# The second attention of a fused transformer kernel: softmax weights as the stationary tile, sums divided per token

## The chip, the cores and the metric

The kernel runs on one core of a Trainium2 chip. A core has a matrix engine (TensorE, PE in the profile; its weight loads are listed apart as PEld), a vector engine (VectorE, DVE), a scalar engine (ScalarE, ACT), a general engine (GpSimd, POOL) and a queue that only issues transfers (SyncE, SP). The engines run at the same time and meet at semaphores. The metric is the device time of one execution in microseconds (us); lower is better.

## The reference

Four layers are computed, each with a gated cross-attention and a gated feed-forward part. The change lies in the cross-attention of the second layer alone:

```python
# B, NQ, D = 32, 56, 128; context: 32 x 1500 x 96; 16 heads of 64
q = (x @ Wq).reshape(B, Nq, h, dh)
k = (context @ Wk).reshape(B, Nk, h, dh)
v = (context @ Wv).reshape(B, Nk, h, dh)
scores = jnp.einsum('bqhd,bkhd->bhqk', q, k) * scale
attn = jax.nn.softmax(scores, axis=-1)
out = jnp.einsum('bhqk,bkhd->bqhd', attn, v).reshape(B, Nq, h * dh)
return out @ Wo + bo
```

`Nk` is 1500 and `Nq` is 56, so each batch has 16 x 56 = 896 pairs of head and query. A pair of head and query is called a token here, as in the title of the change.

## The kernel before

`attention_wide` folds the weights so that keys and values are never projected. `Wq` and `Wk` are merged into one matrix per head, `M`, so a folded query is 96 wide and is multiplied with the raw context; `Wv` and `Wo` are merged into `N` (96 x 128 per head), so the softmax weights are applied to the raw context as well, and the 96-wide result is projected by `N` afterwards.

The 32 batches are taken in two halves of 16, each by one call of `attend_wide`; a half is eight pairs of batches (`NP` = 8), the inner batches of a pair being `s` = 0 and 1. `pairs` writes the first pair out, loops over the middle ones, and writes the last one out. Each pair has 24 steps (12 for each batch); a step is one tile of 125 keys. On PE a step `k` of `body` consists of:

- `chunks`: while `k % 12 < 11`, two (at the eleventh one) products of 128 folded queries with 500 keys of the *next* pair, in PSUM banks 6 and 7. DVE takes their maxima (`chunk_max`, line 1512); the maxima make the shift of the softmax. PE waits before each for the maximum of the one before.
- `score`: six products of 448 columns for the tile two steps ahead (lines 1333 to 1335): keys stationary, all 896 folded queries moving, split in two halves of 448, three products each for precision. ACT exponentiates them into the tile `P` (125 keys x 896 tokens, line 1494).
- `weigh`: two products (line 1347) with the context rows `CN` (125 keys x 97: 96 features and a column of ones) stationary and the 448 columns of `P` moving. The sums stay in banks 4 and 5 as 97 x 896 over twelve steps; row 97 is the softmax's denominator.
- `make_image`: in six of the 24 steps, a product of 500 columns for another layer, in bank 7.
- `project`: once per pair, at step 10, sixteen products of 112 columns (line 1318), `N[0:DC, h, :]` stationary and the normalised sums `UN` moving, into bank 6. `aside` places it. ACT's `out` copies the result into `OT`.

After a batch's twelfth step its sums are normalised: `copy_sums` (ACT, line 1428) copies 97 x 896 into `UE`; SP sends row 97 as 8 x 112 values into spare rows of `qp` (line 1211); DVE's `invert` takes reciprocals (line 1525); SP sends them to device memory (line 1213) and reads them back broadcast over 96 partitions into `RB` (line 1215); POOL's `norm` multiplies (line 1260). Because `project` comes some ten steps later, this runs beside the next batch's steps, except behind the last pair of each half, where `project(NP - 1)` stands alone at the end.

All matmul operands of `weigh` and `project` are float32; the profile shows each such instruction as two records (768 products of `weigh` are 1536 records). The order on each engine is that in which the code is written; nothing is scheduled automatically. Line numbers are those of the profile.

## Time and profile before

| | us |
|---|---|
| median of 3 runs | 4144.75 (4140.34 to 4147.81) |
| the profiled execution | 4137.59 |
| its span, first to last instruction | 4136.0 |
| PE busy in it | 3638.2 (88%) |
| DVE, ACT, POOL busy | 2430.1, 2047.4, 1527.6 |

The steps of the second attention run from about 1209 us of the span to 2529, its last projection to 2546. The busy share of a whole kernel says little, since stages differ; what matters is which engine has no gap where this attention runs, and what one instruction costs there. A matmul record is longer than the time after which the next one starts (they are pipelined): the spacing has to be read from a run of them, as (length of the run - length of one) / (count - 1).

### The profile page before, as it was taken

How to read it: one execution, taken by the hardware profiler on the slowest of the kernel's cores; microseconds unless marked ns; L12 is line 12 of the kernel's file. 1: busy time of each engine (PE TensorE's matmuls, PEld its weight loads, DVE VectorE, ACT ScalarE, POOL GpSimd, SP SyncE). 2: the span in 40 equal slices, each digit the busy share in tenths (PEclk: the TensorE clock that was granted, in tenths of full speed). 3: DMA queues.
4: the chain of work that ended last, by engine and by line, in shares of the span. 5: the costliest groups of instructions: out<-in, count | busy, mean ns of one | idle time of the engine just before them, and what ended most of it. 6: DMA issues, size and time to landing. Idle time of an engine off the chain costs nothing. (4 is left out here: it accounts for less than half of the span.)

```text
span 4136.0 us, 84598 instructions
## 1 busy us (share of the span) xinstructions
PE 3638.2 (88%) x33128; PEld 2481.3 (60%) x33128; DVE 2430.1 (59%) x3802; ACT 2047.4 (50%) x2959; POOL 1527.6 (37%) x1887
## 2 busy tenths in 40 slices
PE   8499999946489999989999997679958799999997
PEld 8367777733366666666666665257733366666664
DVE  7556666543245554515454542467644799999993
ACT  8177777711134443434443442166422377777764
POOL 5265545221423233213323220022201577666651
PEclk9699999968789999999999997889969699999998
DMA  6177777546223332213333220021000566666650
GB/s 188 49 170 178 176 167 175 145 182 235 52 71 90 84 91 81 80 51 87 81 87 87 83 78 26 10 64 46 13 19 16 123 145 144 140 140 147 145 120 15
DMA packets 202294, 421.94 MB, mean 102 GB/s; under 512 B 51993, under 2 KB 108244, under 8 KB 201844
## 3 DMA queue, kind: packets, MB, share of 16 engines
q1 hardware_dynamic: 131524, 327.92, 31.2%
q0 software_dynamic: 34944, 46.10, 5.1%
q10 hardware_dynamic: 35504, 43.39, 3.9%
q8 instruction: 231, 3.78, 0.4%
q14 instruction: 91, 0.75, 0.1%
HBM read 232.39 MB, written 32.56 MB: 64 GB/s over the span
## 5 line engine op out<-in xcount | busy, mean ns | idle before, releaser
L1512 DVE TENSOR_REDUCE L_mp<-ps 128x2 f32<-128x1000 f32 (+1 forms) x352 | 402.4, 1151 | 560.7 <-PE ps L1310 557.3
L1347 PE MATMUL ps<-L_p,L_cn 125*97 125x448 f32 x1536 | 639.2, 538 | 0.0
L1494 ACT ACTIVATE L_p<-ps 125x896 f32<-125x896 f32 x384 | 352.1, 917 | 533.8 <-PE ps L1335 462.5
L2291 DVE TENSOR_REDUCE L_mp<-ps 112x1 f32<-112x500 f32 x726 | 454.2, 667 | 64.5 <-PE ps L2040 64.4
L1333 PE MATMUL ps<-L_qh,L_ch 97*125 97x448 f32 x768 | 384.4, 501 | 0.0
L1347 PEld LDWEIGHTS ps<-L_p,L_cn 125*97 125x97 f32 x1536 | 250.4, 163 | 199.9 <-issue 165.9
L2241 ACT ACTIVATE L_p<-L_p 125x896 f32<-125x896 f32 x256 | 243.3, 950 | 178.6 <-DVE L_p L2308 178.0
L2308 DVE TENSOR_SCALAR L_p<-ps 125x896 f32<-125x896 f32 x256 | 276.5, 1080 | 24.6 <-PE ps L2061 24.5
L920 ACT ACTIVATE L_p<-ps,rk 125x896 f32<-125x896 f32 x256 | 257.7, 1007 | 50.9 <-PE ps L776 46.8
L1334 PE MATMUL ps<-L_ql,L_ch 96*125 96x448 f32 x768 | 282.3, 368 | 0.0
L1335 PE MATMUL ps<-L_qh,L_cl 96*125 96x448 f32 x768 | 280.8, 366 | 0.0
L2040 PE MATMUL ps<-L_ks,L_qs 96*128 96x500 bf16 x768 | 246.3, 396 | 28.2 <-DMA L_qs<-L_q_part 12.4
L1310 PE MATMUL ps<-L_cr,L_qb 96*128 96x500 f32 x672 | 234.7, 427 | 17.3 <-POOL L_qb L1235 17.3
L2061 PEld LDWEIGHTS ps<-L_qs,L_ks 128*128 128x128 bf16 x3072 | 191.0, 99 | 71.5 <-issue 46.4
L776 PEld LDWEIGHTS ps<-L_qs,L_ks 128*128 128x128 bf16 x3072 | 188.0, 98 | 72.9 <-issue 54.6
L2074 PE MATMUL ps<-L_p,L_vs 125*18 125x112 f32 x6144 | 224.1, 264 | 7.2 <-POOL L_p L1923 5.3
L1260 POOL TENSOR_TENSOR L_un<-L_ue,L_rb 96x896 f32<-96x896 f32 x32 | 67.2, 2099 | 424.3 <-DMA L_rb<-L_den 424.3
L692 POOL TENSOR_TENSOR L_k_part<-L_k_rest,L_k_part 128x500 bf16<-128x500 f32 x96 | 109.2, 1139 | 299.4 <-ACT L_k_part L885 299.4
L2061 PE MATMUL ps<-L_qs,L_ks 128*128 128x112 bf16 x3072 | 217.2, 214 | 2.8 <-DVE L_mp L2286 1.5
L776 PE MATMUL ps<-L_qs,L_ks 128*128 128x112 bf16 x3072 | 216.1, 213 | 3.4 <-ACT L_p L920 3.4
L702 POOL DMA_DIRECT2D L_qs<-L_q_part x384 | 214.2, 566 | 7.6 <-DVEq L1042 6.8
L945 DVE COPY L_vs<-ps 125x384 f32<-125x384 f32 x128 | 70.9, 554 | 232.4 <-PE ps L752 232.2
(538 smaller groups left out, 7632.6 us busy)
## 6 DMA issues: line engine op xcount, KB each, us to landing
L_ks<-L_k_part SPq DMA_DIRECT2D x288, 375.0 KB, 6.1
L_ks<-L_k_first SPq DMA_DIRECT2D x96, 375.0 KB, 5.2
moe_w<-in_L_w SPq DMA_DIRECT2D x64, 512.0 KB, 6.6
L_cn<-in_ctxN SPq DMA_DIRECT2D x32, 568.4 KB
cs_ct<-in_ctxT SPq DMA_DIRECT2D x32, 562.5 KB, 4.2
L_cr<-in_ctxT POOLq DMA_DIRECT2D x32, 562.5 KB
L_ch<-in_ctxT POOLq DMA_DIRECT2D x32, 562.5 KB, 4.5
L_raw<-in_ctxT SPq DMA_DIRECT2D x32, 562.5 KB, 5.1
```

Of the source, the lines that this page charges most:

```text
L776: mm = nc.tensor.matmul(SB[n % 2][:, m // 4, m % 4 * 2 * NQ:(m % 4 + 1) * 2 * NQ] .rearrange("p (j q) -> p j q", j=2), KS[b.r % 3][:, k0:k ...
L920: nc.scalar.activation(weights_at[n % 3][0:KP, :].rearrange("p (a n) -> p a n", a=2), SB[n % 2][0:KP], ACT.Exp, scale=rk[:, b.lin(KT, n):b ...
L1333: nc.tensor.matmul(SB[n % 2][:, a, :], CH[s][:, k], QH[s][:, q], start=True, stop=False)
L1334: nc.tensor.matmul(SB[n % 2][:, a, :], CH[s][0:DC, k], QL[s][:, q], start=False, stop=False)
L1335: mm = nc.tensor.matmul(SB[n % 2][:, a, :], CL[s][:, k], QH[s][0:DC, q], start=False, stop=True)
L1347: mm = nc.tensor.matmul(U[:, a, :], CN[s][:, j, :], P[:, n % 2, a * HALF:(a + 1) * HALF], start=(j == 0), stop=(j == KT - 1))
L1494: nc.scalar.activation(two(P[:, n % 2, :]), SB[n % 2], ACT.Exp).then_inc(S["exped"].sem, 1)
L1512: nc.vector.tensor_reduce(mp[:, 2 * k:2 * k + n], ps[:, bank:bank + n, 0:500], AX.X, ALU.max).then_inc(S["chunk_maxed"].sem, 1)
L2040: nc.tensor.matmul(ps[:, CB[pair].start + a, 0:500], QS[b.r % 4][0:96, m * 2 * NQ:m * 2 * NQ + 128], KS[b.r % 4][0:96, m * NK + p * 500:m ...
L2061: mm = nc.tensor.matmul(SB[n % 2][:, m // 4, m % 4 * 2 * NQ:(m % 4 + 1) * 2 * NQ] .rearrange("p (j q) -> p j q", j=2), KS[b.r % 4][:, k0:k ...
L2291: nc.vector.tensor_reduce(mp[:, 2 * c + a:2 * c + a + 1], ps[0:TT, CB[0].start + a, 0:500], AX.X, ALU.max).then_inc(S["chunk_maxed"], 1)
L2308: nc.vector.tensor_scalar(two(P[0:KP, n % 3, :]), SB[n % 2][0:KP], 0.0, -RANGE, ALU.min, ALU.max).then_inc(S["clipped"], 1)
```

## The change

What is stationary and what moves is exchanged in `weigh`. Each step now has seven products (`QT` = 7): 128 tokens of `P` are the stationary tile, and the 97 columns of `CN` move. The sums lie as 128 tokens x 97 in seven places, four in bank 4 and three in bank 5 (`weighed_sum`). So the denominator of a token is on the token's own partition, in column 97:

- `copy_sums` is split: ACT copies the four places of bank 4 (388 columns), DVE the three of bank 5 (291 columns).
- `invert` is one DVE reciprocal of 128 x 7, straight from `UE`; the three transfers of SP, `RB` and the device buffer `den` are gone.
- `norm` on POOL multiplies 128 x 672 with the reciprocals broadcast along the features, into `UT`.
- `project` needs features on partitions, so `turn` transposes the seven tiles of a batch on PE (96 x 128 each, into banks 6 and 7), and `copy_turned` copies them into `UN`, 512 columns by ACT and 384 by DVE. `turn` stands at step 10 (for the batch before) and step 22 (for the first of the pair), behind waits for banks 6 and 7; `project` moves to step 11, ACT's `out` to `n == 13`. At the end of a half `turn` and `copy_turned` stand before the last `project`.

```diff
-    UE = sb("ue", [KA, HQ])
-    UN = sb("un", [DC, H, 2, NQ])
+    UE = sb("ue", [128, QT, KA])
+    UT = sb("ut", [128, QT, DC])
+    UN = sb("un", [DC, 2, HQ])
+    rc = sb("rc", [128, QT])
...
-    U = ps[0:KA, 4:6, 0:HALF]
+    def weighed_sum(t):
+        return ps[:, 4 + t // 4, t % 4 * KA:(t % 4 + 1) * KA]
...
             def norm(i, s):
-                pool.wait_ge(*at("den_in", 32 * i + 16 * s + 16))
-                nc.gpsimd.tensor_tensor(UN[:, :, s, :], heads(UE[0:DC, :]), heads(RB[:, :]), ALU.mult
-                                        ).then_inc(S["u_normed"].sem, 1)
+                pool.wait_ge(*at("den_inverted", 2 * i + s + 1))
+                pool.wait_ge(*at("u_turned", 2 * i + s + 1))
+                nc.gpsimd.tensor_tensor(UT[:, :, :], UE[:, :, 0:DC], rc[:, :].unsqueeze(2).to_broadcast([128, QT, DC]),
+                                        ALU.mult).then_inc(S["u_normed"].sem, 1)
...
+            def turn(i, s):
+
+                pe.wait_ge(*at("u_normed", 2 * i + s + 2))
+                for t in range(QT):
+                    mm = nc.tensor.transpose(ps[0:DC, 6 + t // 4, t % 4 * 128:(t % 4 + 1) * 128], UT[:, t, :],
+                                             core.ident[:, :])
+                mm.then_inc(S["u_turned"].sem, 1)
+
             def project(i):
 
-                pe.wait_ge(*at("u_normed", 2 * i + 3))
+                pe.wait_ge(*at("un_low_copied", 2 * i + 2))
+                pe.wait_ge(*at("un_high_copied", 2 * i + 2))
...
-                for a in range(2):
-                    mm = nc.tensor.matmul(U[:, a, :], CN[s][:, j, :], P[:, n % 2, a * HALF:(a + 1) * HALF],
-                                          start=(j == 0), stop=(j == KT - 1))
+                for t in range(QT):
+                    mm = nc.tensor.matmul(weighed_sum(t), P[:, n % 2, t * 128:(t + 1) * 128], CN[s][:, j, :],
+                                          start=(j == 0 and t % 4 == 0),
+                                          stop=(j == KT - 1 and t in (3, QT - 1)))
...
             def aside(i, k, prev, nxt):
 
-                if k == 10 and prev:
+                if (k == 10 and prev) or k == 22:
+                    pe.wait_ge(*at("img_kept", 6 * i + (3 if k == 10 else 6)))
                     if nxt:
                         pe.wait_ge(*at("chunk_maxed", 2 * CG * i + 2 * CG + groups_by(k)))
+                    else:
+                        pe.wait_ge(*at("chunk_maxed", 2 * CG * i + 2 * CG))
+                if k == 10 and prev:
+                    turn(i - 1, 1)
+                if k == 11 and prev:
                     project(i - 1)
+                if k == 22:
+                    if prev:
+                        pe.wait_ge(*at("out_copied", i))
+                    turn(i, 0)
...
             def body(i, prev, nxt, after):
                 for k in range(24):
+                    if k == 0 and prev:
+                        pe.wait_ge(*at("un_low_copied", 2 * i - 1))
+                        pe.wait_ge(*at("un_high_copied", 2 * i - 1))
...
+            turn(NP - 1, 1)
             project(NP - 1)
...
             def copy_sums(i, s):
                 act.wait_ge(*at("weighed", 24 * i + 12 * s + 14))
                 act.wait_ge(*at("u_normed", 2 * i + s + 1))
-                nc.scalar.activation(two(UE[:, :]), U, ACT.Copy).then_inc(S["u_copied"].sem, 1)
+                nc.scalar.activation(UE[:, 0:4, :], ps[:, 4, 0:4 * KA].rearrange("p (t c) -> p t c", c=KA), ACT.Copy
+                                     ).then_inc(S["u_low_copied"].sem, 1)
...
             def invert(i, s):
-                dve.wait_ge(*at("den_out", 32 * i + 16 * s + 16))
-                nc.vector.reciprocal(dr, dn).then_inc(S["den_inverted"].sem, 1)
+                dve.wait_ge(*at("u_low_copied", 2 * i + s + 2))
+                dve.wait_ge(*at("u_high_copied", 2 * i + s + 2))
+                nc.vector.reciprocal(rc[:, :].unsqueeze(2), UE[:, :, DC:KA]).then_inc(S["den_inverted"].sem, 1)
...
+            def copy_turned(i, s, used):
+                dve.wait_ge(*at("u_turned", 2 * i + s + 2))
+                if used:
+                    dve.wait_ge(*at("projected", i))
+                nc.vector.tensor_copy(UN[:, s, 512:HQ], ps[0:DC, 7, 0:HQ - 512]
+                                      ).then_inc(S["un_high_copied"].sem, 1)
```

How the instructions stand is shown at two places. The first is PE around step 10 of a middle pair, before; `L_p` is `P`, `L_cn` the context rows, `L_un` and `L_N` the operands of the projection, `L_cr` and `L_qb` those of the chunks, and the sizes are those of the result.

```order
L1310 MATMUL ps<-L_cr,L_qb 128x500 [waits L1_chunk_maxed_5]
L1345 REGISTER_ALU
L1347 MATMUL ps<-L_p,L_cn 97x448 [waits L1_exped_5]
L1347 MATMUL ps<-L_p,L_cn 97x448
L1369 REGISTER_ALU
L1316 ISA [waits L1_chunk_maxed_5]
L1318 MATMUL ps<-L_un,L_N 128x112 [waits L1_u_normed_5]
L1318 MATMUL ps<-L_un,L_N 128x112 x15
L1326 ISA
L1333 MATMUL ps<-L_qh,L_ch 125x448 [waits L1_exped_5,L1_max_in1_5,L1_keys_split1_5]
```

The same place with the change (the line numbers are those of the changed file; `L_ut` is `UT`, `ident` the identity):

```order
L1341 MATMUL ps<-L_cn,L_p 128x97 [waits L1_exped_5]
L1341 MATMUL ps<-L_cn,L_p 128x97 x6
L1365 REGISTER_ALU [waits L1_img_kept_5]
L1300 ISA [waits L1_chunk_maxed_5]
L1302 MATMUL ps<-ident,L_ut 96x128 [waits L1_u_normed_5]
L1302 MATMUL ps<-ident,L_ut 96x128 x6
...
L1341 MATMUL ps<-L_cn,L_p 128x97 [waits L1_exped_5]
L1341 MATMUL ps<-L_cn,L_p 128x97 x6
L1308 REGISTER_ALU
L1311 MATMUL ps<-L_un,L_N 128x112 [waits L1_un_high_copied_5,L1_un_low_copied_5]
L1311 MATMUL ps<-L_un,L_N 128x112 x15
```

The two weighings of 448 columns have become seven of 97, the transposes stand where the projection stood, and the projection comes one weighing later, behind waits for the two copies. The second place is SP's queue in the first pair, before:

```order
L1176 DMA L_cn<-in_ctxN 125x1164
L1172 DMA L_raw<-in_ctxT 96x1500 [waits L1_keys_split0_5]
L1176 DMA L_cn<-in_ctxN 125x1164 [waits L1_weighed_5]
L1211 DMA L_qp<-L_ue 8x1x112 [waits L1_u_copied_5]
L1213 DMA L_den<-L_qp 8x112 [waits L1_den_inverted_5]
L1215 DMA L_rb<-L_den 96x896 [waits L1_den_stored_5]
L1172 DMA L_raw<-in_ctxT 96x1500 [waits L1_keys_split1_5]
L1176 DMA L_cn<-in_ctxN 125x1164 [waits L1_weighed_5]
```

and with the change:

```order
L1174 DMA L_cn<-in_ctxN 125x1164
L1170 DMA L_raw<-in_ctxT 96x1500 [waits L1_keys_split0_5]
L1174 DMA L_cn<-in_ctxN 125x1164 [waits L1_weighed_5]
L1170 DMA L_raw<-in_ctxT 96x1500 [waits L1_keys_split1_5]
L1174 DMA L_cn<-in_ctxN 125x1164 [waits L1_weighed_5]
```

The three transfers for the denominators are gone, and the loads of keys and rows follow each other.

## Rows read from the trace of the kernel before

**Rows 1.** The page: busy time of the engines, and one of its groups of instructions.
```profile
PE 3638.2 (88%) x33128; PEld 2481.3 (60%) x33128; DVE 2430.1 (59%) x3802; ACT 2047.4 (50%) x2959; POOL 1527.6 (37%) x1887
...
L1347 PE MATMUL ps<-L_p,L_cn 125*97 125x448 f32 x1536 | 639.2, 538 | 0.0
```

**Rows 2.** Windows: one turn of the pair loop, then the end of the second half.
```profile
core 0: us, PE busy (x) PEld busy (x) DVE busy (x) ACT busy (x) POOL busy (x), PEclk, DMA share, GB/s
1481.24:1561.35 80.11, 80.11 (x322) 54.11 (x321) 41.13 (x53) 32.41 (x45) 23.74 (x17) 1.00 0.31 86
2529.00:2533.50 4.50, 0.00 (x0) 0.00 (x0) 0.85 (x1) 0.92 (x1) 0.00 (x0) 1.00 0.01 2
2534.00:2536.00 2.00, 0.00 (x0) 0.00 (x0) 0.00 (x0) 0.00 (x0) 0.00 (x0) 0.50 0.45 167
```

**Rows 3.** Timeline of PE: two weighings in a row (start, length, engine, line).
```profile
1805.71 3.17 PE L1347 MATMUL ps<-L_p,L_cn 125*97 125x448 f32 x8
```

**Rows 4.** Timeline: sixteen-head projection, then scores and one weighing.
```profile
1561.35 3.72 PE L1318 MATMUL ps<-L_un,L_N 96*128 96x112 f32 x32
1561.35 3.54 PEld L1318 LDWEIGHTS ps<-L_un,L_N 96*128 96x128 f32 x31 [0.19 <-issue]
...
1565.12 0.36 PE L1334 MATMUL ps<-L_ql,L_ch 96*125 96x448 f32 x1
...
1566.14 1.67 PE L1347 MATMUL ps<-L_p,L_cn 125*97 125x448 f32 x4
...
1567.85 0.37 PE L1334 MATMUL ps<-L_ql,L_ch 96*125 96x448 f32 x1
```

**Rows 5.** Timeline: stationary 112 columns with one moving column, and a reciprocal.
```profile
2553.09 3.21 PE L212 MATMUL ps<-J,x2f 128*112 128x1 f32 x32
...
2556.72 0.25 DVE L258 RECIPROCAL rsf<-sdf 112x16 f32<-112x16 f32 x1 [2.81 <-ACT sdf L234]
```

**Rows 6.** Timeline: stationary 97 with moving 128, stationary 128 with moving 97.
```profile
1140.24 0.36 PE L483 MATMUL ps<-L_wka,L_wqt 64*128 64x97 f32 x2
...
1140.13 0.30 PEld L483 LDWEIGHTS ps<-L_wka,L_wqt 64*128 64x128 f32 x2
```

**Rows 7.** Timeline of PE: four transposes of the fourth attention.
```profile
3337.12 0.60 PE L1987 MATMUL ps<-ident,L_ue 128*112 128x128 f32 x4
```

**Rows 8.** Timeline of PE: four transposes of the experts, read with a stride.
```profile
1000.12 0.65 PE L2648 MATMUL ps<-ident,moe_hs 128*128 128x128 f32 x4
```

**Rows 9.** Timeline: end of the second half of the second attention.
```profile
2525.81 3.17 PE L1347 MATMUL ps<-L_p,L_cn 125*97 125x448 f32 x8
...
2529.02 0.92 ACT L1428 ACTIVATE L_ue<-ps 97x896 f32<-97x896 f32 x1 [2.09 <-PE ps L1347]
2529.97 0.66 SPq L1211 DMA_DIRECT2D L_qp<-L_ue  x1
2531.76 0.85 DVE L1525 RECIPROCAL L_qp<-L_qp 8x112 f32<-8x112 f32 x1 [10.48 <-DMA L_qp<-L_ue]
...
2536.78 2.06 POOL L1260 TENSOR_TENSOR L_un<-L_ue,L_rb 96x896 f32<-96x896 f32 x1 [24.27 <-DMA L_rb<-L_den]
...
2538.99 7.14 PE L1318 MATMUL ps<-L_un,L_N 96*128 96x112 f32 x32 [10.01 <-POOL L_un L1260]
2546.17 0.35 ACT L1422 ACTIVATE OT<-ps,vec 128x112 f32<-128x112 f32 x1 [16.23 <-PE ps L1318]
```

**Rows 10.** Groups of instructions, shapes kept apart (count, busy us, mean ns, idle before).
```profile
L1512 DVE TENSOR_REDUCE L_mp<-ps 128x2 f32<-128x1000 f32 x320 | 381.1, 1199 | 535.3 <-PE ps L1310 531.8
...
L1987 PE MATMUL ps<-ident,L_ue 128*112 128x128 f32 x64 | 10.2, 283 | 0.6 <-ACT L_ue L2181 0.6
...
L945 DVE COPY L_vs<-ps 125x384 f32<-125x384 f32 x128 | 70.9, 554 | 232.4 <-PE ps L752 232.2 <-DVE L_q_part L555 0.2
...
L1445 ACT ACTIVATE L_img_o<-ps 128x500 int16<-128x500 f32 x96 | 56.4, 587 | 121.8 <-PE ps L1362 121.8
...
L1512 DVE TENSOR_REDUCE L_mp<-ps 128x1 f32<-128x500 f32 x32 | 21.7, 677 | 25.4 <-PE ps L1310 25.4
```

More of the change, by code:

```diff
@@ L1123, in attend_wide @@
     mc = sb("mc", [128, HB, QT])
-    dn, dr = (qp[DC:DC + 8, n, 0:TT] for n in range(2))
-    RB = sb("rb", [DC, HQ])
     IX, IQ = sb("img_x", [128, 500], I16), sb("img_q", [128, 500], BF16)
@@ L1411, in _ @@
             pairs(pe, body)
[L1412 removed]
+            pe.wait_ge(*at("un_low_copied", 2 * NP - 1))
+            pe.wait_ge(*at("un_high_copied", 2 * NP - 1))
+            turn(NP - 1, 1)
             project(NP - 1)
@@ L1427, in copy_sums @@
                 act.wait_ge(*at("u_normed", 2 * i + s + 1))
-                nc.scalar.activation(two(UE[:, :]), U, ACT.Copy).then_inc(S["u_copied"].sem, 1)
+                nc.scalar.activation(UE[:, 0:4, :], ps[:, 4, 0:4 * KA].rearrange("p (t c) -> p t c", c=KA), ACT.Copy
+                                     ).then_inc(S["u_low_copied"].sem, 1)
+            def copy_turned(i, s, used):
+                act.wait_ge(*at("u_turned", 2 * i + s + 2))
+                if used:
+                    act.wait_ge(*at("projected", i))
+                nc.scalar.activation(UN[:, s, 0:512], ps[0:DC, 6, 0:512], ACT.Copy
+                                     ).then_inc(S["un_low_copied"].sem, 1)
             def load_image(i, c):
@@ L1484, in body @@
                     image_step(i, n, prev, nxt)
-                    if n == 12 and prev:
-                        out(i - 1)
                     if n == 1 and prev:
@@ L1490, in body @@
                         copy_sums(i, 0)
+                        if prev:
+                            out(i - 1)
                     act.wait_ge(*at("scored", 24 * i + n + 1))
@@ L1495, in body @@
                                          ).then_inc(S["exped"].sem, 1)
+                    if n == 11 and prev:
+                        copy_turned(i - 1, 1, False)
+                    if n == 23:
+                        copy_turned(i, 0, prev)
             pairs(act, body)
             copy_sums(NP - 1, 1)
+            copy_turned(NP - 1, 1, False)
             out(NP - 1)
@@ L1506, in _ @@
             dve.sem_inc(S["u_normed"].sem, 1)
+            dve.sem_inc(S["u_high_copied"].sem, 1)
+            dve.sem_inc(S["u_turned"].sem, 1)
             def chunk_max(i, s, k, ahead=False):
@@ L1544, in body @@
                 for k in range(24):
+                    if k == 0 and prev:
+                        copy_sums(i - 1, 1)
+                    if k == 12:
+                        copy_sums(i, 0)
                     if nxt and k % KT < CG:
@@ L1550, in body @@
                         invert(i, 0)
+                    if k == 11 and prev:
+                        copy_turned(i - 1, 1, False)
+                    if k == 23:
+                        copy_turned(i, 0, prev)
                     for c, at_ in enumerate(IMAGE_AT):
@@ L1563, in _ @@
             pairs(dve, body)
+            copy_sums(NP - 1, 1)
             invert(NP - 1, 1)
+            copy_turned(NP - 1, 1, False)
     for name, n in WIDE.items():
```

38 lines of the change are left out of this document (15 added, 23 removed).

## The prediction

> **What bounds the kernel now.** I read the views in the order windows, timeline of PE, groups by shape. The page gives PE 88% of the span, which leaves open where the other 12% lie [rows 1]. The windows answer that for the stage of the change: in one turn of the pair loop, from one projection to the next, PE is busy for 80.11 of 80.11 us at a granted clock of 1.00, while DVE works 41, ACT 32 and POOL 24 us [rows 2]. So inside the loop every nanosecond of PE's instruction stream counts in full, and nothing that the other engines or the queues save there counts at all. The one exception is the end of each half, where PE waits ten microseconds for the normalised sums [rows 9]. The change therefore has to be priced as PE time in the loop, plus or minus what happens at two ends.
>
> **One weighing, before.** PE's busy time is no price, since records overlap. The run of eight records (two weighings, four records each) lasts 3.17 us, and one record 0.538 [rows 1, 3]: (3.17 - 0.538) / 7 = 0.376 us from start to start, 4 x 0.376 = 1.504 us for a weighing. That is 0.84 ns for each of the 448 moving columns; the stationary tile of 97 columns is hidden behind them.
>
> **One weighing, after.** There are 7 products, so 14 records, each with a stationary tile of 128 columns and only 97 moving ones. By moving columns alone a record would take 97 x 0.84 = 0.081 us. The question is whether a new stationary tile can be loaded as fast as that. The nearest row is the projection: 32 records, stationary 96 x 128, 112 moving. From its start to the start of the second score product are 1565.12 - 1561.35 = 3.77 us; for a weighing the same distance is 1567.85 - 1566.14 = 1.71, of which 1.504 are its four records and 0.206 the step to the scores. So 32 records take 3.77 - 0.206 = 3.564, or **0.1114 us each** [rows 4]. Its 112 moving columns would want only 112 x 0.84 = 0.094, so it isn't they that set the pace. A second row says what does: 32 products with a stationary tile of 112 columns and a single moving column still follow each other every (3.21 - 0.28) / 31 = 0.095 us, where a record of that size lasts some 0.28 [rows 5, 10]. Loading costs 0.85 ns for each stationary column, much as moving does, and the next load waits for the one before. For 128 columns that scales to 0.108; the projection, which has just this tile size, shows 0.111, and I take that. Then 14 x 0.1114 = 1.560 us for a weighing, **0.056 more than now**. Exchanging the operands cuts the moved columns from 896 to 679 per weighing, but raises the loaded ones from 194 to 896, and the dearer of the two now is the load. Over 384 weighings: 384 x 0.056 = **+22 us**. With 0.1086 it would be 384 x 0.016 = +6.
>
> The Trainium skill, page "TensorE: Matmul & The Clock Gate", section "LDWEIGHTS (loading the stationary operand)", gives the load as the column count over 1.2, in ns: 0.1067 us for 128 columns; the trace is 4% above it. By the page's figure a weighing would take 1.493 us, the first term would be -4 instead of +22, and the sum below would be about +1.
>
> **The transposes.** These are new on PE: seven for each of 32 batches, one record each, stationary 96 columns and 128 moving ones. The nearest row is four transposes with a stationary 128 x 112 and 128 moving, 0.60 us for four, one record 0.28: (0.60 - 0.28) / 3 = 0.107 [rows 7, 10]. I take 0.11, and 0.77 us for a batch. Thirty of them lie in the pair loops: 30 x 0.77 = **+23 us**, with nothing to hide them, since PE has no gap. The other two lie in the ends, below. Bounds: 0.107 gives 22; 0.123, the spacing of four strided transposes, gives 26 [rows 8].
>
> **The projection** keeps its 32 records with stationary `N` and 112 moving columns; its moving operand is now two pieces of 56, and I cost that at nothing. It moves one step later and adds no instruction.
>
> **New waits on PE.** Three things stand in front of PE's queue now; behind each are the next scores, and behind these ACT. (a) Step 10 and step 22 wait for the chunk maxima and the kept image before `turn`. The chunk of that step is a single one, its maximum takes 0.68 us, and the weighing of 1.56 lies between [rows 10]; an image is made three steps earlier. Cost nothing. (b) `project` at step 11 waits for the two copies of the transposed sums, which can start when `turn` is over: 0.6 us on ACT (500 columns take 0.587), 0.55 on DVE (384 take 0.554), beside the scores of step 12 and the weighing of step 11, together some 2.8 us [rows 10]. Nothing. (c) At step 12, PE waits until ACT has copied the projection out. ACT has `copy_sums` (half the columns it had, about 0.5 of 0.92) and then `out` (0.35) after the projection's end, while PE still has six score products, 1.2 us; that holds too [rows 9]. DVE takes on a copy of 291 and one of 384 columns for each batch, about 1 us, in steps of some 3.3 us where its chunk maximum takes 1.2 [rows 10]. If the covers failed, 32 batches at 0.6 us and a handover of 0.3 would add 29 us.
>
> **SP, POOL and the transfers.** Three transfers and their waits leave SP's queue, so key loads may start earlier; PE waits for none of them in the loop, so that is worth nothing there. POOL's multiply (2.06 us for 896 columns, so some 1.6 for 672) is done by about step 4 and needed at step 10.
>
> **The ends of the two halves.** Now: last weighing's end 2528.98, copy 0.92, transfer out, reciprocal 0.85 at 2531.76, two transfers, multiply at 2536.78 for 2.06, and the projection from 2538.99 to 2546.13, which takes 7.14 us instead of 3.7 because the granted clock, 1.00 (2.4 GHz) up to 2533.5, stands at 0.50 (1.2 GHz) from 2534 on [rows 2, 9]. Together 17.15 us. After: copies 0.55, reciprocal 0.25 (112 x 16 values take that [rows 5]), multiply 1.6, transposes 7 x 0.11 + 0.27 = 1.0, copies 0.6, projection 3.7, and five handovers of some 0.08: 8.1 us. PE would be idle for 2.5 us, work one and be idle for 0.7 more; the projection would start 4.3 us after the last weighing, when before the clock was still at 1.00. So 9 us are saved at each end, 18 in all. If the clock falls all the same, transposes and projection cost 1.9 and 7.1, and it is 12.4: 5 us saved at each end, 10 in all.
>
> **The sum.** +22 + 23 - 18 = **+27 us**. On the profiled execution's own 4137.6 that is 4165; it lies 7.2 below the median of the runs shown, which are what will be compared, so the forecast is 4144.75 + 27 = **4172 us**, 0.65% slower. What a measurement of this kernel can tell from no change is about 0.2%, 8 us.
>
> **The rivals.**
>
> *Faster: the loads hide behind the moving columns.* Place: the 14 records of each weighing. If a load of 128 columns went on beside the 97 moving ones of the product before and didn't wait for the load before it, the spacing would be near 0.08. There is a pair of records of just this shape, stationary 128 and 97 moving, 0.36 us long, so 0.36 - 0.28 = 0.08 apart [rows 6]. A weighing would take 14 x 0.085 = 1.19, the first term would be 384 x -0.314 = -121, and the time 4144.75 - 121 + 23 - 18 = 4029 (4012 at 0.081). It decides from a spacing of 0.1065 down: there the weighing gives back just the 5 us that the other terms cost. Against it: that pair stands between products with 128 moving and 97 stationary columns, so it tells of one record that runs ahead, not of a stream; the two loads beside it are 0.30 us long together, about 0.11 apart [rows 6]; and both long streams of loads run at the load's pace [rows 4, 5]. 0.06. The Trainium skill's page "TensorE: Matmul & The Clock Gate" says, in "Step-by-step: what each phase is for", that the next tile's weights load while this tile's matmul runs; the trace agrees only as far as the matmul is the longer of the two.
>
> *No change: the loads run at a pace below 0.1075.* The one-column stream scales to 0.108 [rows 5], and if `P` loads a little faster than `N`, the weighing costs what it does now. Then only +23 - 18 = +5 remain: 4150, within 8 us of before. 0.08. This is also where the page's load figure leads.
>
> *Slower still: the covers fail.* If the copies of the transposed sums stand in PE's path at each of the 32 batches, +29: 4201. For it: three queues must be on time together. Against it: each has two steps or more. 0.08.
>
> *Slower still: the load of `P` is dearer than that of `N`.* `P` has just been written by ACT and is 125 rows high. At the spacing of the strided transposes, (0.65 - 0.28) / 3 = 0.123 [rows 8], a weighing takes 1.72 us: 384 x 0.218 = +84, 4234. Against it: slices of `P` lie as densely as those of `N`. 0.06.
>
> **How the numbers follow.** The forecast has 0.72. Faster by over 0.2% is the first rival, 0.06; within 0.2% the second, 0.08; slower the forecast and the two others, 0.86. The range goes from 4150, where the load's pace is 0.1075, to 4204, the failing covers at the pace of 0.1114. Outside lie the hidden loads, the dearer loads and the edge of the second rival, some 0.16.
>
> **What would show it.** In the profile after: `weigh` has 5376 records; a run of 14 that starts 1.56 us before the scores behind it bears the main term out, 1.2 the first rival. The turn of the pair loop should be 80.1 + 24 x 0.056 + 2 x 0.77 = 83.0 us, with PE busy throughout. PE idle before `turn` or `project`, or before the chunks of steps 0 and 12, would show a failed cover. At the end of a half the projection should follow the last weighing within 4.5 us and take 3.7. I am wrong in the sign if the turn of the loop is shorter than 80.1.

## The result and the profile after

The changed kernel takes 4169.66 us (median of 4 runs, 4166.71 to 4174.87) against 4143.26 us before (4 runs, 4140.34 to 4147.81); the ratio is 1.0064, with a 95% interval from 1.0047 to 1.0082. It is 26 us slower; the forecast was 27, in a range of 4150 to 4204. The profiled execution took 4174.87 us, span 4173.3, and is the slowest of the four: 37.3 us above the profiled one of before. Of these, 8.1 lie ahead of the first score product of this attention (at 1206.9 us before and 1215.0 after), where both kernels run the same code, so they are not the change's.

The page of the changed kernel answers to [rows 1]; its columns are busy us and mean ns, then the idle time ahead:

```profile
PE 3686.9 (88%) x37192; PEld 2870.0 (69%) x37192; DVE 2464.7 (59%) x3866; ACT 2052.4 (49%) x2991; POOL 1508.2 (36%) x1887
...
L1341 PEld LDWEIGHTS ps<-L_cn,L_p 125*128 125x128 f32 x5376 | 659.2, 192 | 23.9
L1341 PE MATMUL ps<-L_cn,L_p 125*128 125x97 f32 x5376 | 651.8, 273 | 0.0
```

All 5376 records of the weighing products are there. Each has a stationary tile of 128 columns, whose load (PEld) takes 0.192 us, and on this line PEld is now as busy as PE. One turn of the pair loop in the windows of the changed kernel, beside the 80.11 us of [rows 2] and with the same columns (stretch, length, busy time of PE, PEld, DVE, ACT and POOL, PEclk, DMA share, GB/s):

```profile
1500.49:1583.33 82.84, 82.84 (x576) 78.02 (x575) 43.46 (x56) 32.75 (x47) 22.42 (x16) 1.00 0.29 74
```

That is 82.84 us, 2.73 more, with PE still busy from end to end at a granted clock of 1.00: no wait has come in, the instruction stream has become longer. How long a weighing is shows in the timeline of PE, beside [rows 4]. The last line is from a shorter stretch and shows the first two records of the same weighing alone:

```profile
1512.00 0.61 PE L1294 MATMUL ps<-L_cr,L_qb 96*128 96x500 f32 x2
1512.44 1.70 PE L1341 MATMUL ps<-L_cn,L_p 125*128 125x97 f32 x14
1513.92 0.45 PE L1326 MATMUL ps<-L_qh,L_ch 97*125 97x448 f32 x1
1514.21 0.36 PE L1327 MATMUL ps<-L_ql,L_ch 96*125 96x448 f32 x1
...
1512.44 0.36 PE L1341 MATMUL ps<-L_cn,L_p 125*128 125x97 f32 x2
```

Fourteen records take 1.70 us, one 0.273: (1.70 - 0.273) / 13 = 0.110 from start to start. They aren't evenly spaced: the second starts 0.36 - 0.27 = 0.09 us behind the first (0.086 in the trace), the other twelve follow each other every 0.112. From the first of them to the second score product it is 1514.21 - 1512.44 = 1.77 us; before it was 1567.85 - 1566.14 = 1.71. So a weighing with scores behind it costs **0.06 us more**.

The end of the second half in the timeline of the changed kernel, beside [rows 9] (start, length, engine, line):

```profile
2570.85 1.70 PE L1341 MATMUL ps<-L_cn,L_p 125*128 125x97 f32 x14
...
2572.58 0.46 DVE L1556 COPY L_ue<-ps 128x291 f32<-128x291 f32 x1 [0.98 <-PE ps L1341]
2572.58 0.49 ACT L1438 ACTIVATE L_ue<-ps 128x388 f32<-128x388 f32 x1 [0.94 <-PE ps L1341]
2573.15 0.20 DVE L1551 RECIPROCAL L_rc<-L_ue 128x7 f32<-128x7 f32 x1
2573.43 1.31 POOL L1244 TENSOR_TENSOR L_ut<-L_ue,L_rc 128x672 f32<-128x672 f32 x1 [25.16 <-DVE L_rc L1551]
...
2574.89 0.94 PE L1302 MATMUL ps<-ident,L_ut 128*96 128x128 f32 x7 [2.34 <-POOL L_ut L1244]
2575.86 0.59 ACT L1445 ACTIVATE L_un<-ps 96x512 f32<-96x512 f32 x1 [2.78 <-PE ps L1302]
2575.86 0.55 DVE L1563 COPY L_un<-ps 96x384 f32<-96x384 f32 x1 [2.51 <-PE ps L1302]
...
2576.56 6.87 PE L1311 MATMUL ps<-L_un,L_N 96*128 96x112 f32 x32 [0.74 <-ACT L_un L1445]
```

The granted clock there (windows of the same kernel, columns as in [rows 2]; PEclk is the third number from the end):

```profile
2572.00:2575.50 3.50, 1.16 (x11) 1.03 (x11) 0.66 (x2) 0.49 (x1) 1.31 (x1) 1.00 0.00 0
2577.00:2583.00 6.00, 6.00 (x30) 6.00 (x29) 0.00 (x0) 0.00 (x0) 0.00 (x0) 0.50 0.00 0
```

The path is the one that was summed up beforehand: copies at 2572.58, reciprocal, multiply, transposes at 2574.89, copies, projection at 2576.56, 4.0 us after the last weighing's end (2572.55). But the projection takes 6.87 us, and the clock falls to 0.50 at its very start. At the end of the first half the clock is down even earlier, and the transposes are slow too:

```profile
1866.60 1.45 PE L1302 MATMUL ps<-ident,L_ut 128*96 128x128 f32 x7 [2.34 <-POOL L_ut L1244]
1868.79 7.14 PE L1311 MATMUL ps<-L_un,L_N 96*128 96x112 f32 x32 [0.74 <-ACT L_un L1445]
```

**Where the time went**, from the starts of the same records in both traces:

| stretch | before | after | difference |
|---|---|---|---|
| first to last weighing record, first half | 623.5 | 644.3 | +20.8 |
| first to last weighing record, second half | 623.7 | 644.4 | +20.7 |
| last weighing record to end of the projection, first half | 17.7 | 11.9 | -5.8 |
| the same, second half | 17.7 | 11.2 | -6.5 |

That is +41.5 in the loops, -12.3 at the ends, +29.2 in all. It agrees with the 26 us between the medians within their scatter of some 7 us.

### The profile page after: what moved, and what is told of

Same layout as the page of the kernel before. It is cut to its first block and busy times, and to the rows that moved or that the text cites. A ratio compares the mean times of both kernels' runs of the same rounds, so it can differ in the third digit from the quotient of the medians.

```text
span 4173.3 us, 92919 instructions
## 1 busy us (share of the span) xinstructions
PE 3686.9 (88%) x37192; PEld 2870.0 (69%) x37192; DVE 2464.7 (59%) x3866; ACT 2052.4 (49%) x2991; POOL 1508.2 (36%) x1887
## 5 line engine op out<-in xcount | busy, mean ns | idle before, releaser
L1341 PEld LDWEIGHTS ps<-L_cn,L_p 125*128 125x128 f32 x5376 | 659.2, 192 | 23.9
L1341 PE MATMUL ps<-L_cn,L_p 125*128 125x97 f32 x5376 | 651.8, 273 | 0.0
L1326 PE MATMUL ps<-L_qh,L_ch 97*125 97x448 f32 x768 | 321.0, 418 | 0.0
L1182 POOL DMA_DIRECT2D L_ch<-in_ctxT x32 | 17.5, 548 | 599.1 <-PE ps L1328 599.1
```

The source lines that it names most:

```text
L1326: nc.tensor.matmul(SB[n % 2][:, a, :], CH[s][:, k], QH[s][:, q], start=True, stop=False)
L1341: mm = nc.tensor.matmul(weighed_sum(t), P[:, n % 2, t * 128:(t + 1) * 128], CN[s][:, j, :], start=(j == 0 and t % 4 == 0), stop=(j == KT - ...
```

## The experiments

The experiments' times stand beside other executions of the kernel before than the result's, so they are compared by their ratios to it. Its median was 4139.9 us beside the first four runs, 4140.9 beside the next four, 4140.4 beside the last two. The changed kernel's ratio is 1.0064. Four questions are asked: what paces a weighing record, what a transpose costs, what happened to the clock at the ends, and what would make a weighing cheaper.

### Fewer moving columns

```diff
-                    mm = nc.tensor.matmul(weighed_sum(t), P[:, n % 2, t * 128:(t + 1) * 128], CN[s][:, j, :],
+                    mm = nc.tensor.matmul(weighed_sum(t)[:, 48:KA], P[:, n % 2, t * 128:(t + 1) * 128], CN[s][:, j, 48:KA],
```

> The changed kernel with only the last 49 of the 97 context columns moving in each weighing product; the stationary tiles and the number of products are the same, and half of the weighed features is left out of the computation. Theory, the loads of 128 columns set the pace at 0.112 us a record: the moving columns are hidden behind them, so the turn of the pair loop stays at 82.84 us and the time within 5 us of the changed kernel's 4169.7. Rival, the moving columns count too and the 0.112 is their 0.081 with a fixed part on top: 48 columns fewer save 0.040 us a record, 14 x 384 x 0.040 = 217 us, 3953. Second rival, a fixed pace of accumulating into PSUM per written column: the same direction as the first, some 200 us less.

Measured: 4160.57 us, ratio 1.0055 (1.0035 to 1.0074). A weighing in this run's timeline of PE, and its first two records alone:

```profile
1402.47 1.66 PE L1341 MATMUL ps<-L_cn,L_p 125*128 125x49 f32 x14
...
1402.47 0.32 PE L1341 MATMUL ps<-L_cn,L_p 125*128 125x49 f32 x2
```

A turn of the loop in its windows, columns as before:

```profile
1403.96:1486.41 82.45, 82.45 (x576) 77.69 (x576) 43.47 (x56) 32.76 (x47) 22.40 (x16) 1.00 0.28 75
```

The turn is 82.45 instead of 82.84 us. Half of the moved columns gone saves 0.39 us in 24 weighings, 0.016 us each, where the rival wanted 0.56. By the medians the run is 9 us below the changed kernel, more than the 5 that were expected; by the ratios it is 4, and by the loops in the two traces 5.6.

The trace shows where these few us come from. Only the first of the fourteen records is shorter: the second follows it after 0.32 - 0.27 = 0.05 us (0.046 in the trace) instead of 0.086, and the other twelve follow each other every 0.112 as before. Where scores come next, nothing is gained by that, since the way from the first record to the second score product is 1.77 us all the same; where an image product or the transposes come next, in eight of the 24 steps, 0.04 us stay, most of the 0.39. So moving columns don't set the pace from the second record on, and neither does what is written to PSUM.

### More moving columns

```diff
-    CN = [sb(f"cn{s}", [KP, KT, KA]) for s in range(2)]
+    CN = [sb(f"cn{s}", [KP, KT * KA + 31]) for s in range(2)]
...
-        return ps[:, 4 + t // 4, t % 4 * KA:(t % 4 + 1) * KA]
+        return ps[:, 4 + t // 4, t % 4 * 128:(t % 4 + 1) * 128]
...
-                    mm = nc.tensor.matmul(weighed_sum(t), P[:, n % 2, t * 128:(t + 1) * 128], CN[s][:, j, :],
+                    mm = nc.tensor.matmul(weighed_sum(t), P[:, n % 2, t * 128:(t + 1) * 128], CN[s][:, j * KA:j * KA + 128],
```

> The changed kernel with 128 moving columns in each weighing product instead of 97 (the 31 more are values of the next key row, and their sums are never read); the stationary tiles are the same, the result too. Theory, loads set the pace: 128 moving columns want 0.107 to 0.109 us, still under the 0.112 of the load, so nothing changes: 4170 within 5. Rival, moving columns count in full beside the load: 31 x 0.84 ns = 0.026 us a record, 14 x 384 x 0.026 = +140 us, 4310.

Measured: 4168.09 us, ratio 1.0072 (1.0052 to 1.0092), the turn 82.96 us in this run's windows:

```profile
1407.57:1490.53 82.96, 82.96 (x576) 78.15 (x575) 43.46 (x56) 32.74 (x47) 22.42 (x16) 1.00 0.28 74
```

A weighing in its timeline of PE, with 128 columns moving, and its first two records:

```profile
1402.44 1.73 PE L1341 MATMUL ps<-L_cn,L_p 125*128 125x128 f32 x14
...
1402.44 0.38 PE L1341 MATMUL ps<-L_cn,L_p 125*128 125x128 f32 x2
```

A third more moving columns for 0.12 us a turn. The first two records start 0.38 - 0.27 = 0.11 us apart here, the rest again 0.112. The two runs together show that, behind the first, a record of 49, 97 or 128 moving columns costs the same with a stationary tile of 128: the moving columns don't set its pace.

There is a rival that these two runs leave: each record might cost 0.112 whatever the width of its stationary tile. The stream of [rows 5] answers it, with 112 stationary columns and one moving. Here are its last fourteen records in the kernel before:

```profile
2554.79 1.51 PE L212 MATMUL ps<-J,x2f 128*112 128x1 f32 x14
```

One of them lasts 0.237 us in the trace, so they start (1.51 - 0.237) / 13 = 0.098 us apart. That is 0.875 ns for each stationary column, and 128 x 0.875 = 0.112: the pace goes with the columns loaded, at both widths that the traces have. This was the term on which the sign of the forecast rested.

### One transpose instead of seven

```diff
-                for t in range(QT):
+                for t in range(1):
                     mm = nc.tensor.transpose(ps[0:DC, 6 + t // 4, t % 4 * 128:(t % 4 + 1) * 128], UT[:, t, :],
```

> The changed kernel with one of the seven transposes of a batch, six left out (the projection then reads mostly unrelated numbers). My term: six records of 0.109 us for each of 32 batches lie fully on PE's path: 30 x 6 x 0.109 = 20 us in the loops and 1 to 2 in the ends, 4148. Rival, the transposes fill time in which PE would wait for something else: less than 5 us gained, 4166.

Measured: 4145.52 us, ratio 1.0013 (1.0003 to 1.0022), 21 us below the changed kernel, as expected. The turn of the loop in its windows:

```profile
1412.20:1493.73 81.53, 81.53 (x565) 76.73 (x564) 43.27 (x56) 32.76 (x47) 22.42 (x16) 1.00 0.28 76
```

It is 82.84 - 81.53 = 1.31 us shorter by twelve transposes, 0.109 each. Nothing hides them. What all seven cost shows in a step of the changed kernel that has them between weighing and scores:

```profile
1538.55 1.70 PE L1341 MATMUL ps<-L_cn,L_p 125*128 125x97 f32 x14
1540.08 0.93 PE L1302 MATMUL ps<-ident,L_ut 128*96 128x128 f32 x7
...
1541.05 0.37 PE L1327 MATMUL ps<-L_ql,L_ch 96*125 96x448 f32 x1
```

From the first weighing record to the second score product it is 2.50 us, and 1.77 without the transposes: 0.74 for seven, by the means of 28 and 210 such steps. And what is left over before, +0.13%, is the weighings' 19 us and some 3 for the single transposes, less the 15 that the ends give in this run's trace.

### The gaps at the ends filled, in the changed kernel

```diff
+            def filler(n):
+                for _ in range(n):
+                    nc.tensor.matmul(ps[:, 0, 0:448], core.ident[:, :], src[:, 0:448], start=True, stop=True)
...
+            filler(3)
             turn(NP - 1, 1)
+            filler(1)
             project(NP - 1)
```

> The changed kernel with products nobody reads in the gaps at the end of each half: three of 448 columns in front of the last transposes, one in front of the last projection (bank 0). Theory, the clock term of my sum fell because PE idles between the last weighing and the projection: with the gaps filled the granted clock stays at 1.00, the transposes take 0.93 and the projection 3.75 us instead of 6.9 to 7.1, and the products of the next stage start warm: 3.5 + 1 us at each end, 9 less in all, ratio to before 1.0042 instead of 1.0064. Rival, the transposes themselves or the transition bring the clock down: it falls in the projection all the same, and nothing is gained (1.0064), or the fillers delay the transposes and it gets 1 to 2 us slower.

Measured: 4158.37 us, ratio 1.0047 (1.0033 to 1.0060): 7 us less than the changed kernel's ratio; 9 were expected. The end of the second half in this run's timeline; line 1308 is the filler, 1315 the projection:

```profile
2556.82 1.70 PE L1345 MATMUL ps<-L_cn,L_p 125*128 125x97 f32 x14
...
2558.36 2.45 PE L1308 MATMUL ps<-xn,ident 128*128 128x448 f32 x6
...
2560.77 0.97 PE L1302 MATMUL ps<-ident,L_ut 128*96 128x128 f32 x7
...
2561.57 0.92 PE L1308 MATMUL ps<-xn,ident 128*128 128x448 f32 x2
...
2562.47 3.80 PE L1315 MATMUL ps<-L_un,L_N 96*128 96x112 f32 x32
```

The windows of the same run over that stretch, with PEclk at 1.00:

```profile
2558.00:2567.00 9.00, 8.27 (x52) 5.99 (x51) 1.25 (x4) 1.51 (x4) 1.31 (x1) 1.00 0.01 2
```

The clock stays at 1.00, and the projection takes 3.80 instead of 6.87 us. From the start of the last weighing record (2558.25) to the projection's end it is 8.0 us, in both halves, where the changed kernel has 11.9 and 11.2: the clock costs 3.9 and 3.1 us, and their sum is the 7 us of the ratios. Counted from the end of that record, as the forecast did, the path is 7.75 us; the forecast had 8.1, with 1.6 for a multiply that takes 1.31.

### The gap filled in the kernel before

```diff
+            filler(12)
             pe.wait_ge(*at("u_normed", 2 * NP))
             project(NP - 1)
```

> The kernel before with twelve such products of 448 columns (0.75 us each at full clock, 9 us of the 10 that PE idles there) in front of the last projection of each half; nothing else is changed. Theory as above: projection 3.7 us instead of 7.14 at both ends and a warmer start after them, 8 to 9 us less: ratio to before 0.998. Rival: the time there is set by the transfers and the multiply alone and what the projection gains the fillers take: 1.000.

Measured: 4131.82 us, ratio 0.9980 (0.9971 to 0.9989), 9 us less than before. The fillers keep the clock at 1.00 through the wait and the projection, as this run's windows show:

```profile
2524.00:2535.00 11.00, 10.35 (x28) 4.88 (x26) 0.85 (x1) 0.92 (x1) 1.72 (x1) 1.00 0.11 33
2535.00:2540.00 5.00, 3.80 (x32) 3.65 (x32) 0.01 (x1) 0.40 (x2) 0.35 (x1) 1.00 0.00 0
```

In its timeline the projection takes 3.80 us instead of 7.14:

```profile
2535.49 3.80 PE L1322 MATMUL ps<-L_un,L_N 96*128 96x112 f32 x32 [1.14 <-POOL L_un L1260]
```

The projection also starts some 0.2 us later than before, so the ends, from the last weighing record to the end of the projection, are 3.1 and 3.2 us shorter. The other 3 us of the 9 were not followed to their place; behind the second projection the granted clock is 0.74 in the next 2.7 us, where it stayed at 0.50 before.

### Stationary tiles of 64 tokens

```diff
                 for t in range(QT):
-                    mm = nc.tensor.matmul(weighed_sum(t), P[:, n % 2, t * 128:(t + 1) * 128], CN[s][:, j, :],
-                                          start=(j == 0 and t % 4 == 0),
-                                          stop=(j == KT - 1 and t in (3, QT - 1)))
+                    for c in range(0, 128, 64):
+                        mm = nc.tensor.matmul(weighed_sum(t)[c:c + 64, :], P[:, n % 2, t * 128 + c:t * 128 + c + 64],
+                                              CN[s][:, j, :], start=(j == 0 and t % 4 == 0),
+                                              stop=(j == KT - 1 and t in (3, QT - 1)))
```

> The changed kernel with stationary tiles of 64 tokens instead of 128: fourteen products in each weighing, written alternately to partitions 0 to 63 and 64 to 127; the same columns are loaded in all (896, twice), the same result. Theory in its plain form, loads follow one another at 0.85 ns a column whatever half of the array they go to: 28 records at 0.056 us = 1.57 us a weighing, the same as now, 4170 within 8. Rival, loads into the two halves go on side by side, and so do the products: a pair of records every 0.083 us (97 moving columns and little more), 14 x 0.083 = 1.17 us a weighing, 384 x -0.39 = -150 us, 4020. A third outcome, the products are not side by side: 28 x 0.083 = 2.33 us, +290 us, 4460.

Measured: 4185.03 us, ratio 1.0117 (1.0098 to 1.0136), 22 us slower than with tiles of 128. That is none of the three outcomes: by its time the run looks like the third in small, but the trace says otherwise. One step (chunk, weighing, scores) in this run's timeline of PE:

```profile
1418.27 0.62 PE L1294 MATMUL ps<-L_cr,L_qb 96*128 96x500 f32 x2
1418.81 1.39 PE L1342 MATMUL ps<-L_cn,L_p 125*64 125x97 f32 x28
1420.13 0.47 PE L1326 MATMUL ps<-L_qh,L_ch 97*125 97x448 f32 x1
1420.44 0.37 PE L1327 MATMUL ps<-L_ql,L_ch 96*125 96x448 f32 x1
```

And a row of its waits of PE (us in all, times, the longest):

```profile
PE ps L1294 <- issue: 20.8, 10, 2.4
```

Twenty-eight records in 1.39 us, one of them 0.25: 0.042 apart, or 0.084 a pair. The single records come alternately 6 and 77 ns apart. So products in the two column halves of the array do run side by side, loads and all, and the pace is that of the 97 moving columns, as the rival said. Two things take the gain away. First, the way in and out of such a pair costs: from the start of the two chunk products to the second score product behind the weighing it is 1420.44 - 1418.27 = 2.17 us, where the changed kernel has 1514.21 - 1512.00 = 2.21. Only 0.04 of an expected 0.39 is left. Some 0.09 are lost ahead of the records (the first starts 0.32 us behind the chunk product, 0.23 in the changed kernel), the rest behind them; why isn't shown. Second, PE stood still ten times, for 20.8 us in all, in front of a chunk product, with nothing that the profile shows to wait for. Behind the second of these stops, which ends at 1452.90, the granted clock is 0.50 for a while (windows of this run):

```profile
1454.50:1457.50 3.00, 3.00 (x31) 2.24 (x29) 0.34 (x1) 0.00 (x0) 3.00 (x4) 0.50 0.33 122
```

### The same with PE's loop written out

```diff
-            pairs(pe, body)
+            for i in range(NP):
+                body(i, i > 0, i + 1 < NP, i + 2 < NP)
```

> The kernel of stationary tiles of 64 tokens with the loop over the pairs written out on PE instead of a hardware loop. Theory, the 2.2 to 2.7 us that PE stood still in each turn there, just behind the branch back, belong to the branch of a body with twice as many weighing products: written out they are gone, twelve turns of 2.4 us, 29 us less than with the loop, ratio 1.0047 instead of 1.0117, a little under the changed kernel. Rival, the stop is a wait (for the copies or for a maximum) that only shows there: the turn stays at 85.4 us.

Measured: 4151.84 us, ratio 1.0029 (1.0019 to 1.0038): 33 us less than with the loop, and the waits of PE on nothing in front of a chunk product are gone from the list. The turn in this run's windows:

```profile
1408.77:1490.57 81.80, 81.40 (x912) 67.13 (x910) 43.46 (x56) 32.75 (x47) 22.40 (x16) 1.00 0.29 77
```

The turn in the windows of the run before it, with the loop:

```profile
1406.80:1492.23 85.43, 83.26 (x912) 68.00 (x911) 43.46 (x56) 32.76 (x47) 22.36 (x16) 0.98 0.28 74
```

The turn is 81.80 us against 85.43 with the loop, and 1.04 less than the changed kernel, 24 x 0.04. Of the 3.63 us between the two turns, some 2.1 are the stop itself; the other 1.5 are work that runs at half the clock behind it (PEclk 0.98 over the turn, 1.00 without the loop), which the expectation left out. The ten stops are as many as the loops of the two halves have branches back, and they go when the loop does, so they belong to the branch. Whether the length of the body or the form of its tiles brings them on isn't shown: the changed kernel's body, with 14 records of full width instead of 28 of half, has no such stop. This version is faster than the changed kernel, and still slower than before.

### One rounded pass instead of two, in the order of before

The weighing is the largest float32 work of the loop, and each product is two records of 448 columns at 0.84 ns. The scores show another form: inputs rounded to `F32R`, one record of 0.205 for the same 448 columns. This run rounds `P` and the context rows, so the weighed sums have less precision than before.

```diff
-    CN = [sb(f"cn{s}", [KP, KT, KA]) for s in range(2)]
-    P = sb("p", [KP, 2, HQ])
+    CN = [sb(f"cn{s}", [KP, KT, KA], F32R) for s in range(2)]
+    P = sb("p", [KP, 2, HQ], F32R)
...
                     if nxt and s == 0:
                         max_row(i + 1, 0)
+                    if nxt:
+                        pool.wait_ge(*at("weighed", 24 * i + 12 * s + 14))
+                        rows(pool, i + 1, s)
```

> The kernel before, its weighing with P and the context rows held in the rounded float32 form that the scores use (one pass instead of two; the rows are loaded by POOL's queue, which rounds them), so the sums lose precision. Theory, PE's instruction stream alone bounds the loop and a weighing costs its records: 2 products of 448 at 0.205 instead of 4 records at 0.376, 1.09 us less for each of 384 weighings; the turn of the loop falls from 80.1 to 54 us, unless another engine comes to bound it first: 3720. Rival, ACT (0.92 us an exponential plus the image and copies) or the chain of chunk and maximum takes over at some 2.6 us a step: the turn stays at 62 or more, 3850.

Measured: 3919.77 us, ratio 0.9474 (0.9456 to 0.9493), 221 us less: neither 3720 nor 3850. A turn of the loop in this run's windows:

```profile
1371.71:1442.55 70.84, 61.53 (x273) 50.61 (x273) 41.66 (x53) 32.02 (x45) 24.89 (x19) 0.90 0.40 97
```

What PE's loads waited for most in a stretch of 300 us (us in all, times, the longest):

```profile
PEld ps L1364 <- DVE L_mp L1514: 45.1, 26, 2.9
```

PE is busy for 61.5 of 70.8 us only, and the clock is down to 0.90. The place is the image product (line 1364 there) that shares bank 7 with the chunks: it waits for DVE's maximum of the chunks just made, which the long weighing used to cover. My rival had named ACT or the chain of chunk and maximum as a pace of every step; it is this chain, but only in the six steps of a turn that make an image, and the lower clock makes the rest of the loop longer.

### The image product moved into the scores

```diff
+                    if a and between:
+                        between()
                     q = slice(a * HALF, (a + 1) * HALF)
...
                         aside(i, k, prev, nxt)
-                        make_image(i, k, nxt)
                     if k + 2 < 24:
-                        score(i, k + 2)
+                        score(i, k + 2, lambda: make_image(i, k, nxt))
```

> The kernel before with its weighing in one rounded pass (P and the context rows rounded), and the image product moved from behind the weighing into the middle of the next scores. In the one-pass kernel PE stood still some 1.5 us before each of the six image products of a turn, since bank 7 was still being read for the chunk maximum, 18 us in two turns. Theory: three score products (0.6 us) now lie in that wait; but the next chunks wait until ACT has copied the image (0.8 us), with only the other three scores (0.6) in front, so the gain is some 0.4 to 0.6 us an image, 96 x 0.5 = 48 us: 3872. Rival, the chain from chunk over maximum and image to the next chunk is what bounds such a step, and it is only cut by what the scores had hidden badly: less than 20 us, 3905.

Measured: 3883.51 us, ratio 0.9378 (0.9362 to 0.9394): 36 us less, between the theory's 48 and the rival's 20. The waits of PE in a stretch of 300 us, same columns:

```profile
PE ps L1366 <- DVE L_mp L1515: 19.3, 27, 1.4
PE ps L1312 <- ACT L_img_o L1448: 9.6, 27, 0.5
```

The wait for the maximum is down to 0.7 us an image, and the expected second one has appeared, for ACT's copy ahead of the next chunks, 0.36 us an image. With the fillers of the kernel before added:

> The same with the twelve unread products in front of the last projection of each half: 8 to 9 us less than without them, as in the kernel before.

3878.47 us, ratio 0.9365 (0.9350 to 0.9381). The 5 us between the medians of the last two are less than the 8 to 9 expected, and the two intervals overlap. This run's timeline shows a part of the reason. The last projections of the first and of the second half:

```profile
1714.32 5.22 PE L1324 MATMUL ps<-L_un,L_N 96*128 96x112 f32 x32 [1.19 <-POOL L_un L1259]
...
2280.67 3.80 PE L1324 MATMUL ps<-L_un,L_N 96*128 96x112 f32 x32 [1.25 <-POOL L_un L1259]
```

In the first half the clock fell in the middle of the projection (1.00 in the window from 1711 to 1716, 0.50 in that from 1716.6 to 1719), although the same twelve products stood in front of it. Why isn't known. This version is the fastest of all, at the price of rounding named above.

## Why the prediction was right

**The bound.** PE busy for all of 80.11 us in a turn, so only its instruction stream counts: it held after the change too (82.84 of 82.84), and none of the waits that the change adds on PE showed. All the covers that the prediction named were long enough.

**The weighing, +22 forecast, some 19 measured.** The forecast had 0.1114 us a record and 0.056 more a weighing. Where scores follow a weighing, the distance from its first record to the second score product has grown from 1.710 to 1.767 us, by 0.057 (means of 238 and 210 steps). In the quarter of the steps that make an image, only by 0.03. With the transposes' share below taken off, the loops' 41.5 us leave 19. The decision against moving columns as the pace rested on two streams of other lines, and the runs with 49 and with 128 moving columns confirm it from the second record of a weighing on. The first rival, hidden loads at 0.08 and 4029 us, is out, and what the forecast said against its evidence holds word for word: a pair 0.08 apart "tells of one record that runs ahead, not of a stream". The weighings of the changed kernel begin with just such a pair, 0.086 apart, and go on at 0.112. Side by side in two halves of the array the spacing does fall to the moving columns' pace, a pair every 0.084. The Trainium skill's load figure ("TensorE: Matmul & The Clock Gate", section "LDWEIGHTS (loading the stationary operand)"), 0.107 us for 128 columns, would have given no change in this term; the profile has 0.112 between the loads, 5% more, and 14 x 384 x 0.005 is 27 us.

Three of its numbers don't hold, and none of them moves the forecast. The one-column stream of [rows 5] was read with a record of 0.28 us, which is that of another shape; its records last 0.237 and start 0.098 apart, and scaled to 128 columns that is 0.112, not 0.108. The case for the second rival, a pace under 0.1075, rested on this reading. The first rival at a spacing of 0.081 comes to 4008, not 4012. And the failing covers at 0.1114 are 4201, as the rival says, not the 4204 of the range.

**The transposes, +23 forecast, some 22 measured.** A transpose costs 0.109, as the row of the fourth attention said; the run with one in place of seven gave 1.31 us a turn for twelve. Seven cost 0.74 instead of the 0.77 of the forecast, 30 x 0.74 = 22.

**The ends, -18 forecast, -12.3 measured.** This is the term that was mis-sized, and the step of it that failed is the clock: "the projection would start 4.3 us after the last weighing, when before the clock was still at 1.00". In the second half it did start 4.0 us after, but the clock fell there; in the first half the clock was down already during the transposes (1.45 us for seven instead of 0.93). The forecast shows the clock at one end of the kernel before only. At the other, where the last weighing ended at 1835.59, the windows of the same trace show that it was down after 2 us:

```profile
1835.60:1837.50 1.90, 0.00 (x0) 0.00 (x0) 0.00 (x0) 0.92 (x1) 0.00 (x0) 1.00 0.00 0
1837.70:1845.60 7.90, 0.00 (x0) 0.00 (x1) 0.85 (x1) 0.00 (x0) 2.07 (x1) 0.50 0.12 44
```

So the clock fell 2.0 and 5.0 us behind the last weighing before, and 2.6 and 4.3 after, where PE had worked for a microsecond between. In the runs of the changed kernel with 49 and 128 moving columns and with one transpose it was between 1.7 and 4.5 us. The moment varies from end to end whatever stands there, and the transposes can't be told apart from that. The forecast's other case, a clock that falls all the same and 5 us saved at each end, is close to the 5.8 and 6.5 measured. With the gaps filled the ends would have given 9.7 us each, a little more than the forecast's 9, so the clock is the whole of what was missing.

**The sum.** The weighing was 3 us too high, the transposes 1, and the ends promised 5.7 too much: +29 by the traces, +26 by the medians, +27 forecast. The sign and the terms in the loop were right for the reasons given; that the number is closer than its terms is luck, since some 4 us too many met some 6 us too few.

## What to carry to other kernels

When operands of a product are exchanged, price both sides: columns moved and columns loaded cost nearly the same in float32 here (0.84 and 0.88 ns), a hidden load comes into the open as soon as its tile is wider than what moves, and the layout that follows (seven transposes a batch) is paid on the same engine. Read the pace of a stream from the starts of a run of records with the same stationary width, even if it stands in another function, and leave out its first record, which can be quicker. Read the clock at every place where the same wait occurs before a term is built on it. And where one engine is busy from end to end, ask how many passes its products take before asking how they lie: that was worth 5 to 6% here, at the price of precision, where the exchange cost 0.6%.

## What the runs showed of the hardware

- In a stream of products with stationary float32 tiles of 128 columns, a record costs 0.112 us whether 49, 97 or 128 columns move (turns of 82.45, 82.84 and 82.96 us); with tiles of 112 columns and one moving it costs 0.098. Only the first record of a stream goes at the pace of its moving columns: the second follows it after 0.046, 0.086 and 0.11 us with 49, 97 and 128 of them.
- Two products with 64 stationary columns each, in different column halves, start 6 ns apart and pairs follow each other every 0.084 us, so loads go on side by side as well; but some 0.09 us ahead of each weighing and 0.25 behind it are lost, nearly all of the 0.39 that it should save.
- A hardware loop on PE with 28 instead of 14 records in each weighing stood still for some 2.1 us at each branch back (ten, 20.8 us), and behind the stop the granted clock was 0.50 for a while, which cost some 1.5 us more; written out, the stops were gone and the kernel was 33 us faster.
- Behind the last weighing of a half the clock fell after 2.0 and 5.0 us before, with PE idle throughout, and after 2.6 and 4.3 us in the changed kernel, with seven transposes in between. In the changed kernel four unread products of 448 columns at each end kept it at 1.00 through both last projections, which took 3.80 us instead of 7.14 and 6.87; with twelve such products in the rounded kernel it still fell once, in the middle of the projection (5.22 us).
